# Another order of the engines' calls in the first block, the last two heads, the gates and the experts; doubling moved to ScalarE; first loads on two queues

## What is computed

```python
# block one: one head of 256, causal
xn = layernorm(x) * gamma + beta
q, k, v = xn @ qkv[:, :256], xn @ qkv[:, 256:512], xn @ qkv[:, 512:]
x1 = softmax(where(causal, q @ k.T / 16, -inf)) @ v @ o_proj + x
x = layernorm(x + x1)
# block two: 16 heads of 128 with rotary positions, then a mixture of 4 experts, top 2
h0 = layernorm(x) * ln1_w + ln1_b
q, k, v = h0 @ wq + bq, h0 @ wk + bk, h0 @ wv + bv          # per head
q, k = rope(q), rope(k)
h = x + softmax(where(causal, q @ k.T / sqrt(128), min)) @ v @ wo + bo
h1 = layernorm(h) * ln2_w + ln2_b
comb = softmax of the two largest of softmax(h1 @ w_gate)    # 4 weights a row, 2 not zero
m = sum over e of comb[:, e] * (gelu(h1 @ we1[e] + be1[e]) @ we2[e] + be2[e])
out = layernorm(x + h + m)
```

## Time and profile before

| | |
|---|---|
| median of three runs | 1224.1 us (1222.21 to 1226.03) |
| profiled execution | 1224.59 us |
| its span, first to last instruction | 1222.8 us |
| TensorE busy | 1143.8 us (94%) |
| VectorE, ScalarE, GpSimd busy | 868.8 (71%), 733.5 (60%), 642.7 us (53%) |
| granted TensorE clock, mean | 0.968 |
| DMA, mean over the span | 46 GB/s |

### The profile page before, as it was taken

The page is one execution under the profiler, slowest core; times in us unless marked ns, Lnnn a source line. Parts: engine busy times, 40 slices in busy tenths (PEclk is TensorE's granted clock), DMA queues, the critical chain, the costliest instruction groups (busy, mean ns, idle before and its releaser), DMA issues.

```text
span 1222.8 us, 20399 instructions
## 1 busy us (share of the span) xinstructions
PE 1143.8 (94%) x7111; PEld 1034.6 (85%) x7111; DVE 868.8 (71%) x2010; ACT 733.5 (60%) x1563; POOL 642.7 (53%) x514
## 2 busy tenths in 40 slices
PE   6897999999999999999999999999999996768886
PEld 6785879999999999999999999999999885657775
DVE  5856567777777777777777777767777776556765
ACT  3535566666666666666666666766666664344443
...
DMA packets 46300, 56.53 MB, mean 46 GB/s; under 512 B 5940, under 2 KB 29176, under 8 KB 46200
## 3 DMA queue, kind: packets, MB, share of 16 engines
...
...
## 4 chain that ended last, share of the span: by engine, by line
PE 83%; DVE 6%; issue 4%; ACT 3%; POOL 3%; DMA 1%; SPq 1%; POOLq 0%; ACTq 0%; DVEq 0%
PE ps_m L420 51%; PE ps_s L420 20%; PE ps_t L545 10%; DVE rows L1422 1%; PE ps_m L603 1%; DVE pT_lo L1497 1%; ACT prob_b L1028 1%; DVE acc L1412 0%; DVE ps_s L1490 0%; POOL work L2002 0%; POOL work L1998 0%; POOL qk_lo L2009 0%; POOL acc L2022 0%; DVE acc L1591 0%; ACT prob_b L969 0%
## 5 line engine op out<-in xcount | busy, mean ns | idle before, releaser
L1998 POOL TENSOR_TENSOR work<-work,rope 128x512 f32<-128x512 f32 x128 | 166.5, 1301 | 223.6 <-DMA work<-work 223.6
L1035 ACT ACTIVATE pT_hi<-ps_t 128x512 fp32r<-128x512 f32 (+3 forms) x408 | 183.1, 489 | 96.5 <-PE ps_t L545 96.4
L1497 DVE TENSOR_TENSOR pT_lo<-ps_t,pT_hi 128x512 fp32r<-128x512 f32 (+3 forms) x408 | 210.8, 550 | 33.6 <-ACT pT_hi L1035 31.3
L1490 DVE CUSTOM_DVE_ANT_0 ps_s<-ps_s,causal 128x128 f32<-128x128 f32 (+7 forms) x272 | 203.2, 766 | 8.6 <-PE ps_s L420 6.1
L2009 POOL TENSOR_TENSOR qk_lo<-work,qk_hi 128x512 fp32r<-128x512 f32 x128 | 162.9, 1292 | 26.9 <-ACT qk_hi L992 26.8
L2002 POOL TENSOR_TENSOR work<-work 128x512 f32<-128x512 f32 x128 | 167.6, 1309 | 10.0
L1530 DVE SCALAR_TENSOR_TENSOR acc<-ps_m,rinv,acc 128x256 f32<-128x256 f32 x272 | 118.6, 478 | 66.2 <-PE ps_m L420 65.7
L986 ACT ACTIVATE work<-ps_m,bqk 128x512 f32<-128x512 f32 x128 | 88.9, 694 | 120.7 <-PE ps_m L420 120.7
L1028 ACT ACTIVATE prob_b<-ps_s,nmax 128x640 f32<-128x640 f32 (+3 forms) x136 | 130.4, 959 | 26.5 <-DVE nmax L1490 23.4
L420 PE MATMUL ps_s<-qk_hi 128*128 128x384 f32 (+5 forms) x384 | 140.8, 367 | 0.2 <-ACT prob_s L1028 0.2
L420 PE MATMUL ps_m<-pT_hi,v_hi 128*128 128x512 f32 (+2 forms) x384 | 135.1, 352 | 3.7 <-ACT hT_hi L945 2.0
...
## 6 DMA issues: line engine op xcount, KB each, us to landing
work<-work SPq DMA_DIRECT2D x256, 128.0 KB, 2.3
...
```

What stands on the lines that cost most here:

```text
L1035: act.activation(pT_hi[:, slots, cols], t_bank(u, i, j)[:, 0:size * P].rearrange("p (j q) -> p j q", q=P), ACT.Copy).then_inc(t_hi.sem, t_ ...
L1490: dve.tensor_tensor_reduce(s, s, causal[:, T - (i + 1) * P:T], -1.0, ABOVE_ALL, ALU.add, ALU.min, accum_out=nmax[:, u % 2, i:i + 1]).then_ ...
L1497: dve.tensor_tensor(pT_lo[:, slots, cols], t_bank(u, i, j)[:, 0:size * P].rearrange("p (j q) -> p j q", q=P), pT_hi[:, slots, cols].bitcas ...
L1998: pool.tensor_tensor(qs[:, x % 2, :], qs[:, x % 2, :], sin_t[:, c * CH:(c + 1) * CH], ALU.mult).then_inc(sin_done.sem, sin_done.up(u, x))
```

## The change

Five things. All computations stay the same, and so does `head(u)`.

1. The calls in `start` and `ends` stand in another order on all five engines.
2. `double` is a ScalarE activation with scale 2, no longer an addition on GpSimd.
3. Of the first small loads four go out on ScalarE's queue, among its own loads of weights, and SyncE's first loads stand in another order (the first is beta, then x of batch 0).
4. The two gate exponents of batch 1 stand three `middle` calls apart.
5. `end_rows(0, 0)` and `end_rows(0, 1)` stand behind `middle(1, 6)`.

```diff
         @block.scalar
         def _(act):
-            def load_weights():
-                w_attn = A["L0_attn_qkv"].rearrange("(k p) n -> p k n", p=P)
-                act.dma_start(qkv_st[:, :, 0:2 * D], w_attn[:, :, 0:2 * D]).then_inc(w_attn_ld[0], 16)
-                act.dma_start(qkv_st[:, :, 2 * D:], w_attn[:, :, 2 * D:]).then_inc(w_attn_ld[1], 16)
+            def load_weights(m):
+                cols = slice(2 * D, 3 * D) if m else slice(0, 2 * D)
+                act.dma_start(qkv_st[:, :, cols],
+                              A["L0_attn_qkv"].rearrange("(k p) n -> p k n", p=P)[:, :, cols]).then_inc(w_attn_ld[m], 16)
+
+            def load_vec(row, count, name):
+                act.dma_start(vec_st[row:row + count, :], A[name].rearrange("(r n) -> r n", n=P)).then_inc(vec_ld, 16)
+
+            def double(b, c):
+                act.wait_ge(rows_dve.sem, rows_dve.at(b, c, TC - 1))
+                x = flat(acc[:, b, tiles_of(c), :])
+                act.activation(x, x, ACT.Copy, scale=2.0).then_inc(doubled.sem, doubled.up(b, c))
+
+            def load_proj():
                 act.dma_start(op_st, A["L0_attn_o_proj"].rearrange("(k p) n -> p k n", p=P)).then_inc(op_ld, 16)
...
             def start():
-                load_weights()
-                high_proj()
+                load_weights(0)
+                load_vec(2, 2, 'L0_ffn_ln1_w')
+                load_vec(8, 2, 'L0_ffn_ln1_b')
+                load_weights(1)
+                load_proj()
+                load_vec(10, 2, 'L0_ffn_ln2_b')
+                load_vec(4, 2, 'L0_ffn_ln2_w')
                 high_fold(0)
                 high_fold(1)
+                high_proj()
+                high_fold(2)
                 ln_affine(0, 0)
...
         def _(pool):
...
-            def double(b, c):
-                pool.wait_ge(rows_dve.sem, rows_dve.at(b, c, TC - 1))
-                x = flat(acc[:, b, tiles_of(c), :])
-                pool.tensor_tensor(x, x, x, ALU.add).then_inc(doubled.sem, doubled.up(b, c))
...
         def _(sp):
...
             def start():
-                load_vec(8, 2, 'L0_ffn_ln1_b')
-                load_be1()
-                load_vec(10, 2, 'L0_ffn_ln2_b')
+                load_vec(6, 2, 'L0_attn_beta')
+                load_x(0, 0)
+                load_x(0, 1)
+                load_qk_weights(0, 0)
                 load_vec(0, 2, 'L0_attn_gamma')
...
         def _(pe):
...
+                transposes(LAST, 6)
                 expert_in(0, 0)
-                transposes(LAST, 6)
                 transposes(LAST, 7)
```

More of the change, by code:

```diff
@@ L662, in start @@
                 transposes(0, 2)
+                scores(0, 4)
                 project_v(0, 3)
@@ L680, in start @@
                 scores(1, 1)
-                project_q(1, 2)
+                project_q(1, 3)
+                transposes(0, 7)
                 scores(1, 2)
-                transposes(0, 7)
-                project_q(1, 3)
                 first_outputs(0, 1, 1)
+                scores(1, 3)
                 transposes(1, 0)
@@ L731, in start @@
                 transposes(2, 4)
+                scores(2, 7)
                 ln_transpose(3, 0)
@@ L847, in ends @@
                 gate_logits(0, 1)
+                scores(LAST, 4)
+                transposes(LAST, 2)
                 out_project(LAST - 1, 1, 0)
+                scores(LAST, 5)
+                transposes(LAST, 3)
                 scores(LAST, 6)
-                transposes(LAST, 2)
-                transposes(LAST, 3)
                 out_project(LAST - 1, 1, 1)
@@ L1173, in start @@
                 high_p(2, 0)
+                exponent(2, 4)
                 high_p(2, 1)
@@ L1350, in ends @@
                 middle(1, 6)
+                end_rows(0, 0)
+                end_rows(0, 1)
+                middle(1, 7)
                 end_rows(1, 0)
-                middle(1, 7)
                 end_rows(1, 1)
@@ L1711, in start @@
                 row_max(2, 5)
+                ln_apply(3, 1)
                 rotate(3, 1)
-                ln_apply(3, 1)
+                low_p(2, 4)
                 low_o(2, 0)
+                accumulate(2, 0, 0)
                 row_max(2, 6)
-                accumulate(2, 0, 0)
-                low_p(2, 4)
                 rotate(3, 2)
@@ L1906, in ends @@
                 mix(1, 0, 1)
-                ln_apply(6, 0)
                 ln_stats(6, 1)
@@ L1911, in ends @@
                 mix(1, 1, 1)
-                ln_apply(6, 1)
                 mix_bias(1, 2)
@@ L1918, in ends @@
                 mix(1, 3, 1)
+                ln_stats(7, 0)
+                ln_apply(6, 1)
                 mix_bias(1, 4)
```

583 lines of the change are left out of this document (285 added, 298 removed).

## The result

The changed kernel takes 1167.8 us (median of four runs, 1167.2 to 1169.9) against 1223.7 us before (1222.2 to 1226.0): ratio 0.9545, 95% interval 0.9525 to 0.9564, so 56 us or 4.6% less. The forecast was 1179, 1161 to 1206. The profiled execution spans 1165.3 us instead of 1222.8.

What follows compares the result with a forecast made beforehand. TensorE was taken to bound the 790 us loop, leaving its idle time and lower clock outside to gain. Terms of -10 up to 180 us and -35.4 in the tail (+6.6 reserve included) gave -45.4: 1179 us, range 1161 to 1206.

Steps and rivals of the forecast that it cites:

- First block: Up to 180 us: loads -1.2, doubling and small moves -2.8, ScalarE's copies +2, rotation -6, 130 to 180 -2; sum -10.
- the rotation ahead of ln_apply(3,0): Near 119.86 us: TensorE's 5.49 us wait for a bank goes, with the lower clock behind it; -6, from -3 to -9.
- The doubling: From 44 to 105 us: off GpSimd, -2.8 with small moves; four ScalarE calls of 1.1 to 1.3 us delay TensorE, +2.
- Unit 32: 970 to 1059 us: split of O ahead of ln_apply(4, 0), most of the wait moving to transposes(32, 6); -9, 0 to -20.
- Gating: 1059 to 1098 us: the 6.29 us wait behind the gates goes, waits of 3.4, 1.2 and 0.9 us follow; -10, -3 to -18.
- 1098 to 1129: An expert_out between each transpose of rows and its gate logits recovers idle time and clock; -6.
- Experts: 1129 to 1214 us: three causes (gates' second exponent, mean of last rows, end wait) and lower clock mostly go; -17, -12 to -20.
- The reserve of 6.6 us: In the tail after 970 us: new waits that can't be seen in an order of this length, +6.6.
- rival (b): Nothing new arises: no +2 or +6.6, and remaining idle time of 44 to 105 and 130 to 180 goes; about 1165, chance 0.12.
- Rival (c): Experts' bias additions on VectorE collide with GpSimd, TensorE waits and falls to the lower clock; slower, about 1232, chance 0.04.
- (a): Waits move rather than go, GpSimd being busy everywhere; only experts (-17) and rotation (-6) gain; about 1201, chance 0.24.
- (d): The order changes and the time doesn't, each new wait being as long as the old; within 0.3%, chance 0.04.

## Why the prediction was right or wrong

**Bounds and loop: right.** The loop did not move (-0.1), and idle time and clock outside it gave the gain, 1.00 for 0.82 to 0.89.

**First block: wrong, -4.1 for -10.** The step that failed is the sum up to 180 us, which had no term for new waits. Point by point: the rotation ahead of ln_apply(3,0) gave 6.3, as said, with 2.97 us idle from 105 to 130 (under 3 was asked). The loads, put at -1.2, gave 0.5 at vectors() and 0.2 at project_q(4,0): the last vector landed at 11.3 and not at 9.2. The doubling was put at -2.8 (with small moves) and +2, and is -1.7 in this block. The four copies of about 1.06 us on ScalarE cost nothing that the traces show; what went away is a VectorE instruction that waited for a GpSimd instruction of 1.9 us to end. New waits came where the order is as new as behind 970: 1.42 us at 18.02 (low_fold(2) behind split_first(0)), 1.19 at 53.54, 1.93 at 104.94, 1.19 at 125.20, four of about a microsecond after 130. Between first_outputs(1,1,0) and project_q(4,0), where 2 us of idle time should have gone, TensorE idles 7.0 us instead of 4.1. The runs that mended them brought 2.7 and 5.4 us of the missing 6.

**Unit 32: right in kind, too small, -15.1 for -9.** "Most of that wait moves": 2.48 us were left, at transposes(32,5) and not (32,6), and not 3 to 5. The term left ln_apply(4,0) at its length beside GpSimd. In the new place it takes 1.59 us, beside GpSimd's power, and ln_apply(4,1) 1.65, most of it in a pause, for 5.25 and 2.86 before; filling that pause cost 3.0 us in the trace. The prediction foresaw neither meeting, so this part of the gain is luck.

**Gating: -13.4 for -10.** Of the three waits foretold (3.4, 1.2, 0.9) there were 2.06 at transposes(33,6) and 0.96 at out_project(33,0,0). The gates' own length, 11.5 to 4.7 us for parts two and three, was not in the sum; part two runs in GpSimd's 10.33 us of idle time, and part three beside one GpSimd instruction instead of three.

**1098 to 1129: -7.0 for -6.** Right.

**Experts: -17.7 for -17, right in size, with incomplete causes.** Clock 1.00, no wait over 2 us, 68.6 us long, four table loads of 1.28 us hidden. Between the end of the exponent (1095.74) and gelu (1097.05) lie 1.3 us. By the Trainium skill ("ScalarE: Activation LUTs", Rules for kernel authors) it would have been about 2.7; the measurement decides. But the two moves that the term named bring 6.8 us alone: behind one of its "three causes" GpSimd's queue was late as well, by 3.8 us, and the sum had taken each wait as gone with its move. The size is right in part by luck, since moves without a price brought the rest.

**The reserve of 6.6 us: wrong place.** Nothing of that size arose in the tail beyond the waits that the terms had named, and the first block, which had no reserve, fell 6 us short. The result, between the forecast case and rival (b) "nothing new arises" (1165), is thus partly two errors against each other: 6 us too good ahead of 180, and 18 too bad behind 970 (6.6 of reserve, 6.1 in unit 32, 3.4 in gating, the rest in the last two). That the time still lies within the forecast case, 1167 to 1194, is luck: with the first block as forecast it would have been about 1162. Rival (c), collisions of the bias additions, did occur once (6.51 us at 1078.39, VectorE) and cost TensorE nothing. Rivals (a) and (d) are out. Of the signs, ScalarE's copies came out just under the 1.1 to 1.3 us named, and the wait left in unit 32 under the 3 to 5.
